# A four-layer graph network kernel: last row chunk moved as 112 rows and 1, node products and attribute turns put elsewhere

## The reference

```
h1 = mish(concat[x[src], x[dst], edge_attr] @ W1 + b1)
messages = mish(h1 @ W2 + b2)
agg = segment_sum(messages, dst)
u = mish(concat[x, agg] @ W3 + b3)
out = layernorm(x + u @ W4 + b4) * gamma + beta
```

## Time and profile before

| what | us |
|---|---|
| three timed runs | 1270.09, 1265.04, 1260.64 |
| their median | 1265.04 |
| the profiled execution's own time | 1267.67 |
| its span, first to last instruction | 1265.9 |

### The profile page before, as it was taken

How to read it: one execution, slowest core, us unless ns; L and a number is a source line. 1 busy time by engine, 2 the same in 40 slices (tenths; PEclk the granted TensorE clock), 3 DMA queues, 4 the chain that set the end, 5 groups by cost and what they waited for, 6 DMA issues and landing times. The chain is left out here.

```text
span 1265.9 us, 14962 instructions
## 1 busy us (share of the span) xinstructions
PE 1164.8 (92%) x4406; PEld 606.9 (48%) x4411; DVE 802.6 (63%) x1847; ACT 561.3 (44%) x983; POOL 509.1 (40%) x444
## 2 busy tenths in 40 slices
PE   3769887999999998899999999999999979899995
PEld 1134222344444443555555555555555546455652
DVE  5984677656213141387777877777877747846663
ACT  1111322201201111577777777777777724135552
POOL 1000112323433300668866666666666000047660
PEclk9668987999999999899999999999999989999998
DMA  7996996576010111685544444444443020046662
GB/s 270 360 383 219 358 395 213 193 232 215 13 42 15 47 72 75 157 240 113 106 98 94 93 98 93 92 100 93 92 98 61 1 70 1 17 145 199 186 185 76
DMA packets 61108, 177.41 MB, mean 140 GB/s; under 512 B 12741, under 2 KB 13285, under 8 KB 53224
## 3 DMA queue, kind: packets, MB, share of 16 engines
q0 software_dynamic: 32496, 76.65, 25.9%
q1 hardware_dynamic: 28536, 99.80, 21.5%
HBM read 161.36 MB, written 15.05 MB: 139 GB/s over the span
## 5 line engine op out<-in xcount | busy, mean ns | idle before, releaser
L1275 PE MATMUL PS<-w,hidT 128*128 128x512 f32 x696 | 314.4, 595 | 0.0
L1275 PEld LDWEIGHTS PS<-w,hidT 128*128 128x128 f32 x696 | 132.1, 190 | 133.5 <-issue 126.2
L582 POOL DMA_INDIRECT rec_scratch<-rec_src,slot_row x84 | 94.3, 1123 | 252.2 <-DMA rec_scratch<-rec_src,slot_row 204.4
L1106 POOL DMA_INDIRECT pair_sum<-table_j,counts_rec x87 | 147.7, 1698 | 30.6 <-issue 26.2
L1210 ACT ACTIVATE grow<-PS 128x512 f32<-128x512 f32 x174 | 104.1, 598 | 117.8 <-PE PS L1258 83.5
L1098 POOL DMA_INDIRECT pair_sum<-table_i,counts_rec x87 | 88.8, 1020 | 152.5 <-PE PS L1258 74.2
L1371 POOL DMA_INDIRECT u_space<-table_j,rec x87 | 82.1, 943 | 130.9 <-DMA table_j<-agg_rows 93.9
L1215 ACT ACTIVATE grow<-grow,two 128x512 f32<-128x512 f32 x174 | 124.9, 718 | 5.0 <-DVE grow L1156 4.9
L1156 DVE SCALAR_TENSOR_TENSOR grow<-grow 128x512 f32<-128x512 f32 x174 | 120.6, 693 | 6.0
L1220 ACT ACTIVATE grow<-grow 128x512 f32<-128x512 f32 x174 | 109.6, 630 | 5.5
L325 PE MATMUL PS<-ring,mixer 128*32 128x512 f32 x448 | 76.6, 763 | 34.2 <-DMA ring<-basis_rows 14.8
(11 more groups left out here) (234 smaller groups left out, 1757.9 us busy)
## 6 DMA issues: line engine op xcount, KB each, us to landing
ring<-basis_rows SPq DMA_DIRECT2D x56, 1024.0 KB, 9.5
ring<-basis_low SPq DMA_DIRECT2D x30, 256.0 KB, 5.8
w_scratch<-stage SPq DMA_DIRECT2D x112, 32.0 KB
rec_scratch<-ring POOLq DMA_DIRECT2D x2, 1496.0 KB, 14.0
counts_rec<-rec_scratch SPq DMA_DIRECT2D x1, 2992.0 KB, 9.6
rec_scratch<-rec_src,slot_row POOLq DMA_INDIRECT x168, 2.2
root<-L_gnn_root SPq DMA_DIRECT2D x2, 1024.0 KB, 8.9
rows_in<-in_rows_in SPq DMA_DIRECT2D x2, 1024.0 KB, 14.2
```

Of the source, the lines that this page charges most:

```text
L582: nc.gpsimd.indirect_dma_start(out=rec3_dram, out_offset=bass.IndirectOffsetOnAxis(ap=slot_row[:, 1, t:t + 1], axis=0), in_=rec, in_offset ...
L1106: nc.gpsimd.indirect_dma_start(out=pair_sum[:, t % GOT3, :], out_offset=None, in_=tables[0][1], in_offset=bass.IndirectOffsetOnAxis(ap=idx ...
L1275: m = nc.tensor.matmul(o, hidT[:, t % 2, k * P:(k + 1) * P], w2[:, k, :], start=False, stop=(k == KT - 1), skip_group_check=True)
```

## The change

Three edits, independent of each other.

1. The 113 rows of the last chunk move as 112 rows and 1 row, in the load of x (so `x_in` counts to 48) and in the store of the output.
2. `u_half(0, 0)` and `u_half(1, 0)` run in the last two steps of the edge loop, ahead of `seg_sum(85)` and `seg_sum(86)`, in the banks that the finished messages left (banks 7 and 6). The third block starts with `u_half(2, 0)`. The wait for w3 moves into the loop.
3. Only ten of the 22 attribute groups are turned before the loop, through banks 0 to 4 instead of all eight, and copied by ScalarE. Groups 10 to 13 are turned by TensorE in step -1, 14 to 18 in step 0, 19 to 21 in step 1, each time after `pre`, and copied by VectorE (`keep_turn`): the first of each set at the start of VectorE's step, the others after the clamp and product of the tile whose hidden rows come next and ahead of `finish_message` and `finish_hidden`. The clearing of banks 0 to 4 moves to step 2, ahead of `message(1)`, and waits for the last copy. `pre(t)` waits for its group's copy at every fourth tile. The load of w2 waits on SP for the second gather, and its scaling on VectorE moves to step 0, behind the copy of group 14.

```diff
@@ SPREAD = (N - (NT - 1) * P) // 16 * 16
                 sp.wait_ge(sem("x_zero"), 1)
-                sp.dma_start(x_rows[0:N - (NT - 1) * P, NT - 1, :], a["in_x"][(NT - 1) * P:N, :]).then_inc(sem("x_in"), 16)
+                for lo, hi in ((0, SPREAD), (SPREAD, N - (NT - 1) * P)):
+                    sp.dma_start(x_rows[lo:hi, NT - 1, :], a["in_x"][(NT - 1) * P + lo:(NT - 1) * P + hi, :]).then_inc(sem("x_in"), 16)
...
+        U_BANK = (7, 6, 5, 0, 1, 2, 3, 4)
+        U_AHEAD = 2
+        def u_half(n, second, rows):
...
-            none = mes[:, 0, :].bitcast(BF16)[:, 0:D]
+            none = mes[:, 1, :].bitcast(BF16)[:, 0:D]
-            b2_part = [b2_flat[:, (j + 1) * D:(j + 2) * D] for j in range(3)]
+            b2_part = [b2_flat[:, j * D:(j + 1) * D] for j in (0, 1, 3)]
+            TURNS_AHEAD = 10
+            TURNS_AFTER = {-1: range(10, 14), 0: range(14, 19), 1: range(19, N_TURN)}
...
+                sp.wait_ge(sem("got3_i1"), 16)
                 sp.dma_start(w2[:], a["L2_gnn_W2"].rearrange("(k p) o -> p k o", p=P)).then_inc(sem("w2_in"), 16)
...
+                def keep_turn(j):
+                    dve.wait_ge(sem("attr_tp"), j + 1)
+                    nc.vector.tensor_scalar(attr[:, j * D:(j + 1) * D], PS[0:ED, j % NT, :], 1.0, None, ALU.mult).then_inc(sem("attr_late"), 1)
+
                 for s in range(-1, NS + 1):
-                    if s == -1:
+                    late_turns = list(TURNS_AFTER.get(s, ()))
+                    if late_turns:
+                        keep_turn(late_turns.pop(0))
+                    if s == 0:
                         dve.wait_ge(sem("w2_in"), 16)
                         nc.vector.tensor_scalar(w2[:], w2[:], -2.0, None, ALU.mult).then_inc(sem("w2_scaled"), 1)
                     if 0 <= s - 1 < NS:
                         grown(1, s - 1)
                         one_hot(s - 1)
                     if 0 <= s + 1 < NS:
                         grown(0, s + 1)
+                    for j in late_turns:
+                        keep_turn(j)
                     if 0 <= s - 1 < NS:
                         finish_message(s - 1)
...
-                for j in range(N_TURN):
+                for j in range(TURNS_AHEAD):
                     act.wait_ge(sem("attr_tp"), j + 1)
...
                     pe.wait_ge(sem(f"pair3_{t % GOT3}"), 16 * (t // GOT3) + 16)
+                    if t % TURN_GROUP == 0:
+                        attr_kept(t // TURN_GROUP)
...
+                def turn(j):
+                    if j >= NT:
+                        attr_kept(j - NT)
...
                 for s in range(-1, NS + 2):
+                    if s == 2:
+                        clear()
...
                         pre(s + 1)
+                    for j in TURNS_AFTER.get(s, ()):
+                        turn(j)
+                    if s == NS:
+                        pe.wait_ge(sem("w3_in"), 16)
+                    if s >= NS:
+                        assert U_BANK[s - NS] == mes_bank(s - 3)
+                        pe.wait_ge(sem("mish1"), s - 2)
+                        u_half(s - NS, 0, hT)
                     if 0 <= s - 2 < NS:
                         seg_sum(s - 2, chunk if s - 1 < NS else chunk_at(s - 2))
...
-                    sp.dma_start(out[c * P:c * P + rows, :], x_rows[0:rows, c, :]).then_inc(sem("out"), 16)
-                sp.wait_ge(sem("out"), 16 * NT)
+                    for lo, hi in ((0, P),) if c + 1 < NT else ((0, SPREAD), (SPREAD, N - c * P)):
+                        sp.dma_start(out[c * P + lo:c * P + hi, :], x_rows[lo:hi, c, :]).then_inc(sem("out"), 16)
+                sp.wait_ge(sem("out"), 16 * (NT + 1))
...
-                pe.wait_ge(sem("w3_in"), 16)
-                for n in range(KT - 1):
-                    u_half(n, 0)
+                for n in range(U_AHEAD, KT - 1):
+                    u_half(n, 0, hT)
```

More of the change, by code:

```diff
@@ L44 @@
 TAIL = NP - 512
+SPREAD = (N - (NT - 1) * P) // 16 * 16
 def gnn_stack(nc, a, out):
@@ L822, in _ @@
                     if e == 28:
-                        dve.wait_ge(sem("x_in"), 32)
+                        dve.wait_ge(sem("x_in"), 48)
                         norm_stats_dve(dve, 0, x_rows)
@@ L1048, in gnn_stack @@
         b3_col = sb("b3_col", [P, KT], F32, msg)
+        FIRST = 3 * P
+        U_OF = [(k, cols) for cols in (slice(0, FIRST), slice(FIRST, NP)) for k in range(KT)]
+        U_BANK = (7, 6, 5, 0, 1, 2, 3, 4)
+        U_AHEAD = 2
+        def u_half(n, second, rows):
+            k, cols = U_OF[n]
+            for j in range(KT * second, KT * second + KT):
+                m = nc.tensor.matmul(PS[:, U_BANK[n], 0:cols.stop - cols.start], w3[:, j, k * P:(k + 1) * P], rows[:, j - KT * second, cols],
+                                     start=(j == 0), stop=(j == 2 * KT - 1), skip_group_check=True)
+            return m
         p3 = ExitStack()
@@ L1292, in seg_sum, with attr_kept, clear @@
                     m.then_inc(sem("sum_mm3"), 1)
-                pe.wait_ge(sem("rec_in"), 16)
[L1295 to L1305, removed]
+                def attr_kept(j):
+                    if j < TURNS_AHEAD:
+                        pe.wait_ge(sem("attr_T"), j + 1)
+                    else:
+                        pe.wait_ge(sem("attr_late"), j - TURNS_AHEAD + 1)
+                def turn(j):
+                    if j >= NT:
+                        attr_kept(j - NT)
+                    for g in range(TURN_GROUP):
+                        m = nc.tensor.transpose(PS[0:ED, j % NT, g * P:(g + 1) * P], rec[:, TURN_GROUP * j + g, 4:REC], ident[:])
+                    m.then_inc(sem("attr_tp"), 1)
+                def clear():
+                    attr_kept(TURNS_AHEAD - 1)
+                    attr_kept(N_TURN - 1)
+                    pe.wait_ge(sem("none"), 1)
+                    for c in range(NT):
+                        nc.tensor.matmul(PS[:, c, :], none[:, 0:P], none, start=True, stop=False, skip_group_check=True)
+                pe.wait_ge(sem("rec_in"), 16)
+                for j in range(TURNS_AHEAD):
+                    turn(j)
                 pe.wait_ge(sem("w_attr_in"), 16)
                 for s in range(-1, NS + 2):
+                    if s == 2:
+                        clear()
                     if s == 0:
@@ L1561, in _ @@
             def _(pe):
-                def u_half(n, second):
-                    k, cols = U_OF[n]
-                    for j in range(KT * second, KT * second + KT):
-                        rhs = aggT[:, j - KT, cols] if second else hT[:, j, cols]
-                        m = nc.tensor.matmul(PS[:, U_BANK[n], 0:cols.stop - cols.start], w3[:, j, k * P:(k + 1) * P], rhs,
-                                             start=(j == 0), stop=(j == 2 * KT - 1))
-                    if second:
-                        m.then_inc(sem("u_mm"), 1)
                 def turn_rows(tag, src, c, bank):
@@ L1640, in _ @@
                 pe.wait_ge(sem("agh_tc"), 1)
-                u_half(KT - 1, 0)
+                u_half(KT - 1, 0, hT)
                 pe.wait_ge(sem("agh_tc"), NT)
                 for n in range(KT):
-                    u_half(n, 1)
+                    u_half(n, 1, aggT).then_inc(sem("u_mm"), 1)
                 for n in range(KT, NU):
-                    u_half(n, 0)
-                    u_half(n, 1)
+                    u_half(n, 0, hT)
+                    u_half(n, 1, aggT).then_inc(sem("u_mm"), 1)
                 pe.wait_ge(sem("w4_in"), 16)
```

9 lines of the change are left out of this document (3 added, 6 removed).

## The result

| | before | changed | |
|---|---|---|---|
| median of the runs, us | 1265.12 (4 runs) | 1247.54 (4 runs) | ratio 0.9861 [0.9817, 0.9905] |
| lowest to highest, us | 1260.64 to 1270.09 | 1244.67 to 1250.90 | |
| profiled execution / its span, us | 1267.67 / 1265.9 | 1247.6 / 1245.7 | |

What follows compares the result with a forecast made beforehand. TensorE, busy for 92% of the span, was taken as the bound. Store -8.6, load -2.5, edge MLP start +4.3 and loop's end -7.6 gave -14.4 us: 1253.3 profiled, 1250.6 against the median; range 1241 to 1260.

Steps and rivals of the forecast that it cites:

- The store: End of the kernel: splitting the output's 113 rows over the DMA engines gains 8.6 us, range 7.6 to 9.9.
- The load of x: Sort stage: splitting the load's 113 rows ends one DMA engine's lag and gains 2.5 us, range 0 to 3.3.
- Early waits of TensorE for pieces are hidden: Sort stage: VectorE is the bound at first, so TensorE's early waits for pieces of the bases cost nothing.
- If that wait is the rest of the one engine's lag, 3.3 us go: Sort stage: TensorE's 3.33 us wait at 87.42 goes if one engine's lag causes it; nothing if all engines' load does.
- The start of the edge MLP: Late attribute turns: 4.4 us won at the front, 7.2 lost behind, 1.5 for the clock: 4.3 lost, ends 1.6 and 7.7.
- the clock's 1.5: Start of the edge MLP: half-speed clock after TensorE's standstill costs 1 to 2.5 us more, taken as 1.5.
- With w2 in its way the add may need 1.5 more: Ahead of `pre(0)`: tile 0's add lands 4.9 us after issue, perhaps 1.5 us later beside w2's load.
- The loop's end: Two half products moved ahead of the last `seg_sum`s gain 7.6 us, range 5.0 to 7.9; 5.0 if the clock falls.
- A: Rival: start costs only 1.6 us, sort stage gives 3.3, store 9.9; sum -19.2, 1245.8 us; chance 0.2.
- B: Rival: sort stage gives nothing, start costs 5.5, clock falls over the barrier; sum -8.1, 1256.9 us; chance 0.25.
- C: Rival: the edge loop falls into a slower rhythm; at 0.25 us a tile the sum is +7, 1272 us; chance 0.05.
- my case: The prediction's main case for the whole kernel: 14.4 us faster, 1250.6 us against the median; chance 0.5.

Runs made afterwards that it cites:

- e1_store: The kernel before, with only the store of the last chunk cut into 112 and 1 rows: 1275.91 us, ratio 0.9926.
- e2_load: The kernel before, with only the load of x's last chunk cut into 112 and 1 rows: 1275.83 us, ratio 0.9931.
- e3_tail: The kernel before, with only the two half products of u moved into the edge loop's last steps: 1273.77 us, ratio 0.9919.
- e7_extra113: The kernel before with x's load split, plus an added transfer of 113 rows of x behind piece 11 of the bases: 1284.24 us, ratio 1.0029.
- e8_extra112: The same as e7_extra113, but with 112 rows in the added transfer, as the control: 1270.88 us, ratio 0.9924.
- e5_w2_later: The changed kernel, with w2's load waiting for the landed pair of tile 0 instead of the second gather: 1267.41 us, ratio 0.9887.
- e11_w2_at_once: The changed kernel, with w2 loaded at once instead of waiting for the second gather: 1248.81 us, ratio 0.9864.
- e10_18_at_once: The changed kernel with 18 groups turned ahead, the last four in step -1, and w2 loaded at once: 1236.53 us, ratio 0.9767.
- e4_no_turns: The changed kernel without its third edit (all 22 groups turned ahead, w2 loaded at once and scaled first): 1256.78 us, ratio 0.9784.
- e6_w2_held: e4_no_turns with the load of w2 waiting for the second gather: 1238.87 us, ratio 0.9777.
- e9_18_ahead: The changed kernel with 18 groups turned ahead, four in step -1, and w2 waiting for tile 0's landed pair: 1257.15 us, ratio 0.9811.

## Why the prediction was right, and where it wasn't

- **The store** (-8.6): right. 9.5 between the profiles and in e1_store, near the upper end of 9.9.
- **The load of x** (-2.5, range 0 to 3.3): 10.5 us went. That one engine's lag reaches to the wait at 87.42 was seen rightly. In the runs one row less in the load took 9.1 to 10.1 us off the stage (e2_load against e1_store and e3_tail), and one row more in an added transfer put 13.8 on (e7_extra113 against e8_extra112). The Trainium skill, "DMA: Bandwidth & Descriptors", section "Why a DMA increments its semaphore by 16 and not by 1", states that a transfer gets the largest number of engines up to 16 that divides the length of its slowest dimension, so one for 113 rows and sixteen for 112. By this rule, the store's 27 GB/s and these runs agree. "Early waits of TensorE for pieces are hidden" held in the main: of 7.84 us of them 1.5 were left at the 14th mix. The step that failed is "If that wait is the rest of the one engine's lag, 3.3 us go": it priced the wait by its own length. The wait gave 3.0, the stretch ahead of it 3.1 and the stretch behind it 2.9. In both stretches the clock was at 0.50 for longer in the kernel before than in the changed one. On one chip (e3_tail against e2_load) the stretch ahead gave nothing, the wait of 5.68 us 5.4, and the stretch behind it 3.3. So the part ahead of the wait can be chance of this pair, and the part behind it came in both. That the wait is what held the clock down there is argued from the order of the rows; no run moved the clock alone. That all eight waits added up, 11.2 us, lie near the 10.5 is luck: in e1_store, e3_tail and e7_extra113 the waits of the stage add up to 13.4, 16.2 and 17.9 us, for 9.1, 10.1 and 13.8 of the stage.
- **The start of the edge MLP** (+4.3, measured +8.8, above the range's end of 7.7): kind right, size off, and all of the error ahead of `message(0)`. Forecast 9.35, 19.15 and 31.45 us after the first turn for `pre(0)`, `message(0)` and `message(1)` (the clock's 1.5 included in the last); measured 12.98, 24.78 and 35.97. The first failed step is "With w2 in its way the add may need 1.5 more": the addition went out at 501.10, as forecast 4.4 us after the first turn, and landed 8.5 us later, where 4.9 had been taken, and `pre(0)` followed at once. e5_w2_later, which moves w2 away, has `pre(0)` at 9.7: that step is shown. The second is the clock: behind 7.16 us of standstill, `pre(0)` ran at half of it (1.09 + 2.07 in place of 0.60 + 1.16, so 1.4 more), and copy 10 came ahead of VectorE's clamp; hidden rows 2.7 us later in place of 0.5. From `message(0)` to `message(1)` the working held: 11.2 us against 12.3 forecast, with 3.67 us of waiting for the last copies, and the clock stayed up. The range's lower end, 1.6, is by its own terms 4.3 - 1.5 - 1.5 = 1.3; nothing hangs on it.
- What neither the forecast nor the first theory saw: mending w2 alone does not help. Held longer, it holds b2's rows too; loaded at once, it leaves the queue of late groups as it was. The +4.15 us at `message(0)` are, against before: -0.8 (`pre(0)` earlier), +1.4 (its half clock), +1.3 (the rest of the hidden rows' delay, copy 10 and its neighbours), +2.2 (turns 14 to 18 ahead of the message; without turns 15 to 18 the scaling of w2 behind copy 14 would still have ended at 521.40). The +4.7 behind it are +1.5 (turns 19 to 21), +3.7 (wait for the last copies), +0.9 (clearing), -1.4 (`message(0)` at full clock, 3.70 in place of 5.06). Emptying the front gave only 0.8, since the pair was the next bound. That the late groups of steps 0 and 1 are the cause is shown by e11_w2_at_once against e10_18_at_once, which differ in nothing but which groups are late, and by e4_no_turns; how much each of turns, copies, clearing and scaling costs alone was not tried.
- **The loop's end** (-7.6, range 5.0 to 7.9): right, 8.1, and 0.5 more at the barrier. The clock stayed at 1.00 over the standstill ahead of the third block, as taken.
- **The rivals.** A had the sort giving all and the start costing 1.6; B had the sort giving nothing. The truth was outside both: the sort gave three times "all", the start cost more than B's 5.5 (a figure for which B gives no terms). C is refuted: `message(1)` to the last `seg_sum` is 486.3 us against 486.2. That the total lies between my case and A is owed to errors of 8.0 and 4.5 us with opposite signs.

## What to carry to other kernels

- A transfer like the one of 113 rows should be split so that nearly all of it has a row count that sixteen divides, early loads above all: its cost is not one late tile but a lag that shows at other transfers up to 80 us later. Only 113 against 112 rows was measured here.
- Where such a lag is seen, do not price it by the last wait alone, nor by all waits added up. Early waits can be made up again, and a late one can cost more than its length by the clock behind it. Put the same product of two kernels side by side through the stage, and see where the difference grows.
- A wait put into an engine's list holds everything behind it. The wait ahead of w2 also held three small loads, and in two experiments these, not the addition that was suspected, were what TensorE waited for. Where the view names no releaser, list all semaphores that the code waits for at that place.
- Work moved into a gap must find room on every engine of its chain. Moving twelve turns out of an idle stretch that something else bounded, into the queue ahead of the first messages, cost 9 us. Moving two products into a gap that nothing was waiting for won 8 to 10 together with what it took off the block behind.

## What was unexpected of the hardware

- One transfer of 113 rows in the middle of a stage cost 13.4 us over the same with 112, more than the 8.6 us for which, by the estimate from the store's 27 GB/s, it keeps its engine busy. SP's next four issues took 8.89 us in place of 1.39.
- Beside a load of 1 MB an addition by indirect DMA landed 8.5 us (changed kernel), 6.7 and 7.0 us (e6_w2_held) after its issue, against a median of 4.9. Three loads of 1 KB each, issued right behind the megabyte on its queue, were in 7.0 us (e5_w2_later) and 10.7 us (e9_18_ahead) after the last of their issues; in e11_w2_at_once, where the first of them was issued 4.2 us after w2, it was 2.0 us.
- Standstills of nearly the same length left the clock at either level: behind 3.67 us in the changed kernel the clock was at 1.00 and `message(1)` took 3.60 us; behind 3.69 us in e5_w2_later it was at 0.50, the clearing took 2.29 in place of 1.25 and `message(1)` 5.42. What decides was not tried.
- The chips differ: the kernel before took 1265 to 1284 us, and the node stretch, 226.3 us on one, took 243 to 244 on that of the first set. A difference of two kernels must be taken on one chip.
